# A fused attention and feed-forward block: attention run in units of two steps instead of single steps

## The reference

```python
xn = layernorm(x)
q = rope((xn @ Wq) as 32 heads of 64);  k = rope((xn @ Wk) as 8 heads of 64);  v = xn @ Wv (8 heads)
scores = q @ k.T / 8            # 4 query heads share one k/v head
allowed = (j <= i) & (i - j < 128)
attn = softmax(where(allowed, scores, -inf)) @ v
x = x + attn @ Wo + ffn(xn)     # ffn: Hadamard, gate/up, silu(gate) * up, Hadamard, down; inner size 1024
```

## Time and profile before

| | |
|---|---|
| median of 3 runs | 1424.41 us (1423.75 to 1425.84) |
| profiled execution, its own time | 1425.82 us |
| its span in the trace | 1424.1 us |
| mean granted TensorE clock | 0.989 of 2.4 GHz |
| busy: PE, PEld, DVE | 1339.1 us (94%), 1043.0 us (73%), 904.1 us (63%) |
| busy: ACT, POOL | 752.2 us (53%), 677.3 us (48%) |
| feed-forward sums added to the result (L858), first and last of 8 | 90.0 and 1298.3 us |

### The profile page before, as it was taken

The page is one execution under the profiler, slowest core; times in us unless marked ns, Lnnn a source line. Parts: engine busy times, 40 slices in busy tenths (PEclk is TensorE's granted clock), DMA queues, the critical chain, the costliest instruction groups (busy, mean ns, idle before and its releaser), DMA issues. The chain is left out here.

```text
span 1424.1 us, 34061 instructions
## 1 busy us (share of the span) xinstructions
PE 1339.1 (94%) x12776; PEld 1043.0 (73%) x12776; DVE 904.1 (63%) x1496; ACT 752.2 (53%) x2685; POOL 677.3 (48%) x719
## 2 busy tenths in 40 slices
PE   6799888999999999999999999999999999999998
PEld 3576666867778777877778777787777877687776
DVE  5657664477755677457773677547785477744775
ACT  2346554266643666356662666526663366634665
POOL 5226533066531765236651565416653166523664
PEclk9899989999999999999999999999999999999999
DMA  6224341433322342323414244043332234231332
GB/s 230 68 59 127 105 141 52 119 89 93 119 76 80 105 119 85 103 61 96 138 51 134 57 113 129 31 119 90 98 113 82 82 100 118 83 107 49 91 112 60
DMA packets 71554, 138.35 MB, mean 97 GB/s; under 512 B 15328, under 2 KB 29152, under 8 KB 71136
## 3 DMA queue, kind: packets, MB, share of 16 engines
q1 hardware_dynamic: 70400, 135.46, 32.8%
q10 hardware_dynamic: 992, 0.73, 0.2%
HBM read 73.21 MB, written 12.58 MB: 60 GB/s over the span
## 5 line engine op out<-in xcount | busy, mean ns | idle before, releaser
L485 POOL TENSOR_TENSOR e_sb<-e_sb,rinv 128x512 f32<-128x512 f32 x256 | 266.1, 1040 | 356.3 <-DVE rinv L830 336.5
L592 ACT ACTIVATE e_sb<-S,negmax 128x128 f32<-128x128 f32 x1024 | 362.1, 368 | 134.2 <-DVE negmax L825 134.2
L709 DVE TENSOR_TENSOR prod<-PROJ,rope_sb 128x1024 f32<-128x1024 f32 x160 | 195.0, 1219 | 58.6 <-PE PROJ L898 49.7
L602 ACT ACTIVATE pt_sb<-TR 128x512 f32<-128x512 f32 x256 | 153.2, 599 | 141.4 <-PE TR L1051 138.0
L1040 PEld LDWEIGHTS S<-k_stack,q_stack 64*64 64x64 f32 x5632 | 172.6, 134 | 74.7 <-issue 53.0
L1040 PE MATMUL S<-k_stack,q_stack 64*64 64x128 f32 (+2 forms) x5632 | 214.7, 276 | 0.0
L592 ACT ACTIVATION_READ_ACCUMULATOR e_sb<-S,negmax 128x1 f32 x1024 | 211.0, 206 | 0.0
L818 DVE COPY_PREDICATED S<-diagonal_key,S 128x512 f32<-128x512 int8 x192 | 132.9, 692 | 116.1 <-PE S L1040 115.1
L1051 PE MATMUL TR<-ident,e_sb 128*128 128x128 f32 x1024 | 169.0, 288 | 33.2 <-POOL e_sb L485 23.8
L825 DVE TENSOR_REDUCE negmax<-S 128x4 f32<-128x512 f32 x256 | 176.9, 691 | 8.8
L493 POOL TENSOR_SCALAR_AFFINE_SELECT p_cur<-pt_sb 128x512 f32<-128x512 f32 x256 | 163.2, 637 | 22.7 <-ACT pt_sb L602 21.2
(11 more groups left out here) (96 smaller groups left out, 2657.1 us busy)
## 6 DMA issues: line engine op xcount, KB each, us to landing
q_stack<-qy SPq DMA_DIRECT2D x512, 64.0 KB, 2.0
wq_ring<-wq_split_d SPq DMA_DIRECT2D x56, 512.0 KB, 3.7
wo_ring<-wo_split_d SPq DMA_DIRECT2D x56, 512.0 KB, 4.0
k_stack<-ky SPq DMA_DIRECT2D x256, 64.0 KB, 3.1
x_in<-x SPq DMA_DIRECT2D x8, 512.0 KB, 4.5
wq_split_d<-wq_ring SPq DMA_DIRECT2D x8, 512.0 KB, 3.1
wo_split_d<-wo_ring SPq DMA_DIRECT2D x8, 512.0 KB, 3.8
out<-acc SPq DMA_DIRECT2D x8, 512.0 KB, 4.9
```

The lines of the kernel that those rows point to most:

```text
L485: nc.gpsimd.tensor_tensor(e, e, r, ALU.mult).then_inc(norm_done, 1)
L592: last = nc.scalar.activation(e_sb[:, n % 2, r, :], s_heads(n, 1)[:, r, :], ACT.Exp, bias=negmax[:, n % 2, r:r + 1], accum_out=rowsum[:, n ...
L602: nc.scalar.activation(pt_sb[:, n % 4, :, :], TR[:, :, :], ACT.Copy).then_inc(t_copied, 1)
L709: nc.vector.tensor_tensor(prod[:, 2 * part:2 * part + 2, :], both, rope_sb[:, :, :], ALU.mult).then_inc(prod_done, 1)
```

## The change

Attention goes in 17 units. Unit u has on PE: scores of steps 2u and 2u+1, transposes of step 2u-2, the filler of slot 2u, transposes of step 2u-1, the filler of slot 2u+1, and the mixing of steps 2u-2 and 2u-1 together. So the mixing of a step now follows in the unit after its scores.

The mixing is cut by query halves a (0: queries 0 to 63 of the tile; 1: queries 64 to 127). Its first part is `pt_sb` times a V, 128 rows deep, 128 moving columns: V of tile i-1 for a=0, and for a=1 a `v_mix` whose first 64 keys come from tile i and the others from tile i-1. What is then missing is only keys 0 to 63 for a=0 and keys 64 to 127 for a=1: the second part has 64 rows and 128 moving columns, on 64x64 tiles. Tile 0 needs no second part and no mask. Half a=0 goes to the first half of `O`, half a=1 to the first half of the bank `TR`. So the first transposes of a unit wait for `o_split`, which DVE gives once it has read the mixing of the unit before. `o_copy` and `o_low` are two instructions each, of 256 columns.

`v_mix` is made by DVE, two copies per tile. The q job 2 moves from the first slots to the feed-forward part, between gate and up of hidden tile 4. The x fillers move from slot 25 to slot 24, `xn` gets its own buffer, and is written tile by tile at slots 20 to 23. ACT's copies of fillers come after the exponentials of the same slot. DMA issues keep their number; `stack_k(1)`, `save_wq` and `load_wq` stand at other places of SP's list.

```diff
-    ROPE_SLOTS = {("q", 2, 0): (0, 1), ("q", 3, 0): (4, 5), ("q", 4, 0): (7, 8), ("k", 1, 0): (10, 11),
-                  ("q", 5, 0): (13, 14), ("q", 6, 0): (17, 18), ("q", 7, 0): (21, 22), ("k", 0, NEXT): (27, 28),
-                  ("q", 0, NEXT): (31, 32)}
+    ROPE_SLOTS = {("q", 3, 0): (0, 2), ("q", 4, 0): (4, 6), ("k", 1, 0): (8, 10), ("q", 5, 0): (12, 14),
+                  ("q", 6, 0): (16, 18), ("q", 7, 0): (20, 22), ("k", 0, NEXT): (26, 28), ("q", 0, NEXT): (30, 32)}
...
+        O_half = [O[:, 0:2 * P].rearrange("p (s m q) -> p s m q", s=2, m=2),
+                  TR[:, 0:2, :].rearrange("p s (m q) -> p s m q", m=2)]
```

On GpSimd:

```diff
+                for u in range(UNITS):
+                    if u:
+                        normalise(2 * u - 1)
+                    for n in (2 * u - 2, 2 * u - 1):
+                        for kind, m, row in rope_jobs(b, n, 1):
+                            rotate(row, kind, m)
+                    for n in (2 * u - 2, 2 * u - 1):
+                        if n >= 0 and n % TT:
+                            mask(n)
+                    if u < UNITS - 1:
+                        normalise(2 * u)
+                    if u < TT - 1:
+                        value_step(u + 1)
```

On ScalarE:

```diff
+                for u in range(UNITS):
+                    if u:
+                        t_copy(2 * u - 2)
+                    if u < UNITS - 1:
+                        exps(2 * u)
+                    read_fillers(2 * u)
+                    if u:
+                        t_copy(2 * u - 1)
+                    if u < UNITS - 1:
+                        exps(2 * u + 1)
+                    if u == UNITS - 2 and b + 1 < BATCH:
                         load_table(ACT.Silu)
+                    read_fillers(2 * u + 1)
+                    if u:
+                        o_copy(u - 1)
```

On VectorE (behind this, in each unit, the fillers of both slots):

```diff
+                for u in range(UNITS):
+                    if u:
+                        inverse_sum(2 * u - 1)
+                    if u >= 2:
+                        o_low(b, u - 2)
+                    if u < UNITS - 1:
+                        fold(2 * u)
+                        fold(2 * u + 1)
+                    if u < TT - 1:
+                        value_mix(u + 1)
+                    if u < UNITS - 1:
+                        inverse_sum(2 * u)
+```

On TensorE (`transposes`, `values_mixed` and the loop over units):

```diff
+                    if n >= 2 and n % 2 == 0:
+                        pe.wait_ge(o_split, (b * STEPS + n) // 2)
                     for r in range(REP):
                         last = nc.tensor.transpose(TR[:, r, :], e_sb[:, n % 2, r, :], ident[:, :])
...
-                    terms = [(v_sb[:, 0, :], p_cur)]
-                    if i:
-                        terms = [(v_sb[:, i - 1, :], pt_sb), (v_step[:, i - 1, :], p_cur)]
...
+                    pe.wait_ge(t_copied, b * STEPS + 2 * pair + 2)
...
+                        for a in range(2):
+                            v = v_mix[:, i - 1, heads] if i and a else v_sb[:, max(i - 1, 0), heads]
+                            for odd in range(2):
+                                last = nc.tensor.matmul(O_half[a][odd * D:(odd + 1) * D, s, :, :], v,
+                                                        pt_sb[:, (2 * pair + s) % 4, odd:REP:2, a * HP:(a + 1) * HP],
+                                                        start=s == 0, stop=False)
+                    pe.wait_ge(v_stepped, b * (TT - 1) + min(2 * pair + 1, TT - 1))
...
+                            for odd in range(2):
+                                for a in range(2):
+                                    half = slice(a * HP, (a + 1) * HP)
+                                    last = nc.tensor.matmul(O_half[a][odd * D:(odd + 1) * D, s, :, :],
+                                                            v_step[half, i - 1, heads], p_cur[half, (2 * pair + s) % 4, odd:REP:2, half],
+                                                            start=False, stop=s == 1)
...
+                for u in range(UNITS):
+                    if u < UNITS - 1:
+                        scores(2 * u)
+                        scores(2 * u + 1)
+                    if u:
+                        transposes(2 * u - 2)
+                    fill(2 * u)
+                    if u:
+                        transposes(2 * u - 1)
+                    fill(2 * u + 1)
+                    if u:
+                        values_mixed(u - 1)
```

More of the change, by code:

```diff
@@ L114, in attention_and_ffn_block @@
         USES += [("v", b, 0, 0), ("v", b, 0, 1)]
-        for n in range(LAST_SLOT + 1):
+        for n in range(2 * UNITS):
             USES += fillers(b, n)
@@ L389, in _ @@
                                  ).then_inc(x_loaded, 16)
-                stack_k(1)
-                if not b:
-                    save_wq(2)
-                load_wq(b, 4)
+                for m in (4, 5):
+                    if not b:
+                        save_wq(m - 2)
+                    load_wq(b, m)
                 for n in range(2, NKV):
@@ L412, in _ @@
                         load_wo(b, n - 1)
+                    if not b and n >= 3 and n <= 5:
+                        save_wq(n + 2)
+                    if n == 4:
+                        load_wq(b, 7)
+                    if 5 <= n <= 6 and b + 1 < BATCH:
+                        load_wq(b + 1, n - 5)
                 if not b:
@@ L636, in _, with read_fillers @@
                 v_copy(1)
-                for n in range(LAST_SLOT + 1):
+                def read_fillers(n):
                     for kind, row, m, part in fillers(b, n):
@@ L740, in _ @@
             row_rstd(0)
-            row_normalised(0)
+            for t in range(TT):
+                row_normalised(0, t)
             dve.wait_ge(w_hi, 1)
@@ L1094, in _, with fill @@
                 pe.wait_ge(ffn_added, b + 1)
-                for n in range(LAST_SLOT + 1):
-                    if n < STEPS:
-                        scores(n)
-                    if 2 <= n <= STEPS + 1:
-                        transposes(n - 2)
+                def fill(n):
                     for kind, row, m, part in fillers(b, n):
```

175 lines of the change are left out of this document (80 added, 95 removed).

## The result

The changed kernel takes **1433.51 us** (median of 8 runs, 1429.01 to 1435.0) against 1425.01 us (8 runs of before on the same chip). The ratio is 1.0053, 95% interval 1.0039 to 1.0067: slower by half a per cent, 33 us more than the 1400 forecast. The time is inside the range, the sign is wrong. The profiled execution took 1434.78 us, with a span of 1433.1.

What follows compares the result with a forecast made beforehand. PE was taken to bound the kernel, busy 166.3 of 172.1 us. Per sequence -5.2 (columns) -5.3 (tile shapes) -5.8 (old waits) +13.2 (new waits) = -3.1 us, -25 for eight: median 1400 us, range 1372 to 1440.

Steps and rivals of the forecast that it cites:

- The step that failed: PE's granted clock is 1.00 throughout, the level of 2.4 GHz, and no gap is long enough to change that.
- idle time of PE: Per sequence, new waits of 13.2 us on PE against the 5.8 us of old waits that go.
- PE's work at full clock: Per sequence, 5.2 us less mixing streaming and 5.3 us less for changes of tile shape.
- Columns and tile shapes: Mixing's second part takes 0.215 us a step for 0.43, 5.2 us less; fewer shape changes, 5.3 us less per sequence.
- Rival A: Mixing's first part: 128-row weight loads show, a step costs 0.39 us more, 1500 us, slower; chance 0.10.
- The wait for TR: A unit's first transposes start 1.70 us after the mixing; PE waits 0.24 or 0.45 us, 0.35 in the mean.
- Rival B: Chain through ACT and DVE at its upper end, 2.0 us: 36 us more, 1436 us, slower; chance 0.15.
- The special places: New PE waits per sequence: 3.9 us at the start, 2.9 at slot 24, 2.3 in the last unit.
- Rivals C and D: C: waits mostly hidden, 1360, chance 0.12; D: shape changes not saved, special waits smaller, within 3 us of 1424, chance 0.08.

Runs made afterwards that it cites:

- unread_work: The changed kernel plus 16 matmuls that nothing reads ahead of each of the two long waits, in each sequence but the last: 1413.49 us.
- last_unit: The changed kernel with, in a sequence's last unit, the q filler ahead of the first transposes and the Silu table load behind the copies of `O`: 1409.92 us.
- tr_first: The changed kernel with ACT and DVE taking the half in bank TR first, each half counted, and the transposes waiting for that half alone: 1380.21 us.
- all_three: The changed kernel with the edits of `tr_first`, `last_unit` and `x_behind_wo` together: 1359.86 us.
- x_behind_wo: The changed kernel with the second x transposes of a sequence moved from slot 24 to slot 25, behind the output projection: 1429.11 us.
- pause_long: The kernel before plus one wait per sequence: behind the transposes of step 18, PE waits for the exponentials of step 20: 1449.72 us.
- pause_short: The kernel before plus one wait per sequence: ahead of the scores of step 20, PE waits for the exponentials of step 19: 1434.44 us.
- early_v: The changed kernel with `v_mix` ahead of remainders and folds on DVE, and `v_step` ahead of rotation and masks on POOL, in the first units: 1461.46 us.
- third_v: `all_three` with only the third tile's `v_step` and `v_mix` made earlier: 1359.62 us.

## Why the prediction was wrong

**The step that failed** is in the part on what bounds the kernel: "The granted clock is 1.00 throughout, the level of 2.4 GHz, and I expect no gap long enough to change that." The sum itself put in gaps of 2.9 us at slot 24 and 2.3 us in the last unit, and 3.9 at the start, and gave them their own length alone. The trace of the kernel before already spoke against it: its mean clock is 0.989, and in its first sequence half clock follows long waits, one of them this:

```profile
147.77 1.12 PE L1051 MATMUL TR<-ident,e_sb 128*128 128x128 f32 x4 [2.44 <-POOL e_sb L485]
```

```profile
148.00:150.00 2.00, 2.00 (x8) 1.71 (x8) 1.97 (x5) 0.60 (x1) 1.23 (x2) 0.50 0.22 88
```

How much of the miss of 33.5 us is the clock? The 26 us of full clock missing are too much, since they count time in which PE stands idle. In PE's busy time it is 2.6 us in the period of the table below, and 16 us over the six periods behind the first (942.0 us busy against 6 x 154.27); the same six are 13.2 us shorter in `unread_work`, which has more work and the same order. So the clock is about half of the miss and its largest term. Without these 16 us the changed kernel would be near 1417 us, an estimate, and the sign would have been as forecast.

**Per period**, forecast and measured (622.44 to 793.12 against 622.71 to 791.56):

| term | forecast | measured | from |
|---|---|---|---|
| idle time of PE | +7.4 (13.2 for 5.8) | +8.1 (13.85 for 5.76) | windows |
| PE's work at full clock | -10.5 | -8.8 (154.27 for 163.09) | mean of `last_unit`'s three periods at 1.00 |
| clock | 0 | +2.6 (156.83 - 154.27) | as above |
| sum | -3.1 | +1.8 | |

`last_unit` has the same PE records as the changed kernel. One of its three periods at full clock is shown above; the others are busy 154.28 and 154.29 us. The table is for one period. Of the seven, the first is 7.2 us shorter than before (187.13 against 194.33) and the other six together 10.4 longer. Outside the periods, the first stretch up to the first addition is 3.5 us longer (93.55 us against 90.0) and the part behind the last one 2.2 us. Together these are the 9.0 us between the two spans. Why the first period gained, no run shows.

- **Columns and tile shapes:** nearly right. The first part takes 0.054 us a record between neighbours, 0.22 per four, as forecast; the second part of a pair with 8 records 0.27 (678.93 to 679.20), where 0.215 was put. In the sum for the changes of tile shape, the list for a unit (0.10, 0.18, 0.09, 0.09, 0.14) adds to 0.60 us, 1.20 for two and not 1.10. Of the two terms of 5.2 and 5.3 us together 8.8 came. `tr_first`, without waits, has two units in 13.14 us, where the working had 13.1. So little of the missing 1.7 us lies in the plain units. Up to 0.7 of it goes with the waits: in `all_three`, which has fewer of them, the same 1817 records at full clock are busy 153.55 us, not 154.27. Where the last 1.0 lies, the runs don't tell.
- **Rival A** (weight loads show) did not happen: between neighbours no record of the first part took 0.066 us or more. Only the first four of a mixing take 0.27 us (677.90 to 678.17), which has the change of tile shape in it.
- **The wait for TR:** the mechanism held, in nearly every unit, but the chain is 1.84 us, not 1.70, so 0.57 and 0.34 us, not 0.45 and 0.24. The copies were right (ACT 0.38 each, DVE 0.42 and 0.41, together 0.66 and 0.75 us); of the handovers the last, from DVE to PE, was 0.15 us and not 0.05. In all 77.0 us, where "35 to 45 us in all" stood in the text. About 44 of it are plain units (12 x 0.455 x 8), 18 the last ones, which that sentence had not counted, and the first sequence alone has 19.6 where a later one has 8.3. Rival B, which needed 1.9 us, was closer than I thought, but did not decide.
- **The special places:** start 3.7 (0.16, 0.57, 1.52 and 1.42) against 3.9, slot 24 2.6 (0.57 for TR and 2.01) against 2.9, last unit 2.30 against 2.3, and the 12 other units 5.2 against 4.1. The sum of all waits came within 0.7 us.
- **Rivals C and D:** C's condition (waits hidden) is not what happened, but `all_three` makes it so by three small edits, and lands at 1359.9 us; C's number was 1360. That is no confirmation of its working, since the clock takes part in both.

**What stays open:** which of two equal waits is followed by half clock. Runs and rows show equal waits (2.65 us; 2.01 us; 1.53 and 1.42 us) with both outcomes, and that taking one away can bring the fall at another. That the others moved in time relative to what decides it is argued, not shown. Open too are the first stretch, the first period and the end, which no run looks at by themselves.

## What to carry to other kernels

When a sum adds or removes waits of the engine that bounds the kernel, list the long ones by themselves (2.0 to 2.3 us here, and the pair of 1.5 and 1.4), and give each a possible half-clock stretch behind it (1.3 to 2.8 us here, in some or all of its occurrences); read the granted clock in windows of 2 us, since means of 0.98 over a period look harmless. A wait that can't be removed may be filled with work that nothing reads, and that is quickly tried. And look first for the half of a chain that the waiting engine does not need: two instructions in the other order, with a count for each, were worth 53 us (1433.51 to 1380.21).

## What was not expected of the hardware

- Half clock behind waits of 2.0 and 2.3 us in the changed kernel (six of seven sequences), and behind two waits of 1.5 and 1.4 us shortly after one another in `x_behind_wo` (six of the seven from the second on). A wait of 2.65 us in `pause_long` had it in 4 of 6 cases; the waits of up to 1.3 us that `pause_short` adds from the second sequence on had it in none.
- 16 products that nothing reads, once per sequence, made the kernel `all_three` 15.4 us faster (1359.86 to 1344.46).
- A DVE copy of 64 x 512 from SBUF to SBUF takes 0.41 us with POOL idle, and 1.00 to 1.43 us beside POOL's instructions with two inputs of 128 x 512 (`early_v`, `third_v`).
